# Projections of the first cross-attention in half chunks, one to a tile, and ten tiles of its softmax sums on POOL

## The reference

```python
cq = heads(ci @ cq_w, NH, CHD)            # 16 heads of 8
ckv = encoder_outputs @ ckv_w
ck, cv = jnp.split(ckv, 2, axis=-1)
ck, cv = (heads(ck, NH, CHD), heads(cv, NH, CHD))
cctx = sdpa(cq, ck, cv, causal=False)     # softmax(cq ck / sqrt(8)) cv
```

## Time and profile before

| | us |
|---|---|
| median of 3 runs (lowest, highest) | 1729.5 (1728.61, 1733.84) |
| the profiled execution | 1730.58 |
| its span | 1728.8 |
| PE busy | 1527.6 (88%) |
| DVE busy | 976.1 (56%) |
| ACT busy | 621.7 (36%) |
| POOL busy | 473.5 (27%) |
| loop of the first cross-attention, in the span | 242.8 to about 658 |

### The profile page before, as it was taken

How to read it: one execution, slowest core, us unless ns; L and a number is a source line. 1 busy time by engine, 2 the same in 40 slices (tenths; PEclk the granted TensorE clock), 3 DMA queues, 4 the chain that set the end, 5 groups by cost and what they waited for, 6 DMA issues and landing times.

```text
span 1728.8 us, 22247 instructions
## 1 busy us (share of the span) xinstructions
PE 1527.6 (88%) x8274; PEld 795.9 (46%) x8275; DVE 976.1 (56%) x1410; ACT 621.7 (36%) x997; POOL 473.5 (27%) x377
## 2 busy tenths in 40 slices
PE   7667569999999988998996789999899989999998
PEld 3234225455454444445663335555434345555344
DVE  6775456666666735412334657677542667777541
ACT  1132226655656652003553223333313233333221
POOL 1540025665665761000000104333000123343000
PEclk9877569999999998998998889999999999999999
DMA  6000512232232214002311000110012100000000
GB/s 234 0 1 3 117 36 66 70 90 65 70 90 57 62 28 127 0 0 72 108 71 53 32 0 27 31 33 19 2 33 68 58 9 28 27 28 19 3 0 22
DMA packets 37829, 80.42 MB, mean 47 GB/s; under 512 B 5564, under 2 KB 23756, under 8 KB 37708
## 3 DMA queue, kind: packets, MB, share of 16 engines
q1 hardware_dynamic: 37712, 78.91, 15.7%
HBM read 56.79 MB, written 0.92 MB: 33 GB/s over the span
## 4 chain that ended last, share of the span: by engine, by line
PE 73%; DVE 17%; ACT 4%; issue 3%; POOL 1%; DMA 0%; SPq 0%; DVEq 0%; POOLq 0%; ACTq 0%
PE psum L1722 20%; PE psum L2242 7%; DVE WA L1386 5%; PE psum L1888 4%; PE psum L1914 3%; PE psum L1939 3%; PE psum L2189 3%; PE psum L1861 3%; DVE WBZ L1625 3%; PE psum L2057 3%; PE psum L1874 3%; PE psum L2217 2%; PE psum L2219 2%; PE psum L2250 2%; PE psum L2234 2%
## 5 line engine op out<-in xcount | busy, mean ns | idle before, releaser
L1386 DVE TENSOR_REDUCE WA<-psum 112x2 f32<-112x1000 f32 x192 | 230.5, 1200 | 141.3 <-PE psum L1888 141.1
L953 ACT ACTIVATE WBZ<-psum 125x896 f32<-125x896 f32 x192 | 176.0, 917 | 158.0 <-PE psum L1914 122.2
L1116 ACT ACTIVATE WA<-psum,y_bias 125x448 f32<-125x448 f32 x192 | 121.4, 634 | 253.5 <-PE psum L2237 253.5
L740 POOL TENSOR_TENSOR XN<-XN,WBZ 125x896 f32<-125x896 f32 x96 | 199.9, 2082 | 15.3 <-ACT WBZ L953 1.8
L2242 PE MATMUL psum<-WA,ctxN 125*128 125x448 f32 x384 | 179.1, 550 | 0.4 <-ACT WA L1116 0.4
L1613 DVE TENSOR_REDUCE y_max<-psum 112x1 bf16<-112x375 f32 x256 | 129.8, 538 | 65.3 <-PE psum L2219 65.0
L769 POOL TENSOR_TENSOR XN<-const,y_max 112x896 bf16<-112x896 f32 x32 | 53.7, 1679 | 335.2 <-DVE y_max L1613 326.5
L1888 PE MATMUL psum<-WA,XB 32*112 32x500 f16 x384 | 84.6, 435 | 39.8 <-DVE WA L1386 39.8
L1914 PE MATMUL psum<-R 100*125 100x224 f16 x768 | 116.3, 274 | 0.0
L760 POOL TENSOR_SCALAR ctxT<-ctxT 128x375 f32<-128x375 f32 x32 | 56.1, 1754 | 199.1 <-ACT std L839 196.5
L1625 DVE RECIPROCAL WBZ<-WBZ 128x224 f32<-128x224 f32 x68 | 105.1, 1547 | 1.2
(11 more groups left out here) (257 smaller groups left out, 2630.1 us busy)
## 6 DMA issues: line engine op xcount, KB each, us to landing
R<-WA SPq DMA_DIRECT2D x192, 93.8 KB, 2.2
ctxT<-in_ctxT SPq DMA_DIRECT2D x12, 750.0 KB, 4.3
R<-in_ctxT SPq DMA_DIRECT2D x12, 750.0 KB, 5.5
WA<-in_ctxT SPq DMA_DIRECT2D x8, 750.0 KB, 4.1
ctxT<-in_ctxT SPq DMA_DIRECT2D x32, 187.5 KB
ctxN<-in_ctx SPq DMA_DIRECT2D x32, 187.5 KB
WBZ<-in_x_w SPq DMA_DIRECT2D x4, 1024.0 KB, 6.4
WA<-in_x_wq SPq DMA_DIRECT2D x2, 1024.0 KB, 6.7
```

Of the source, the lines that this page charges most:

```text
L740: nc.gpsimd.tensor_tensor(z_sum[b % 2][0:TK, :], first[0:TK, :], z_p[t % 4][0:TK, :], ALU.add)\
L953: nc.scalar.activation(z_p[t % 4][0:TK, :].rearrange("p (k n) -> p k n", k=2), psum[0:TK, s:s + 2, 0:2 * GC], ACT.Exp, scale=float(CHD0) * ...
L1116: nc.scalar.activation(y_pT[t][0:TK, g * HALF:(g + 1) * HALF], bank[2 + u % 3][0:TK, 0:HALF], ACT.Exp, bias=y_bias[0:TK, bass.ds(b * NT + ...
L1386: V.tensor_reduce(z_mx[0:PR, r:r + 3:2, c], psum[0:PR, 4:6, 0:PC], AX_X, ALU.max)\
```

## The change

Each projection is cut into two halves, side 0 and side 1, one to a tile: the values in tiles 0 to 5, the keys in tiles 6, 7, 9, 10 and 11 and, for the last half, between the first and the second group of `sums`. Side 0 stands behind the tile's `scores`, side 1 ahead of them, and only side 1 signals ACT. ACT empties the bank ahead of the exponent of the next tile. `turn_maxima` keeps tile 8 for itself. `UNITS_AT` goes from 5 to 4, so each unit comes one tile later. `SUMS` goes from 7 to 9: POOL adds tiles 0 to 9 with nine adds, PE has three groups of sums, and the waits of `exps` for a free buffer change with it. The diff, cut to its core:

```diff
-        UNITS_AT = 5
-        VALUES_AT = {0: 0, 1: 1, 3: 2}
-        KEYS_AT = {4: 0, 6: 1, 9: 2}
-        LOW_AT = {5: 0, 7: 1, 10: 2}
+        UNITS_AT = 4
+        VALUES_AT = {0: (0, 0), 1: (0, 1), 2: (1, 0), 3: (1, 1), 4: (2, 0), 5: (2, 1)}
+        KEYS_AT = {6: (0, 0), 7: (0, 1), 9: (1, 0), 10: (1, 1), 11: (2, 0), 12: (2, 1)}
         TURN_AT = 8
-        SUMS = NT - 5
+        SUMS = NT - 3
...
+                elif b > 0 and t < SUMS - 7:
+                    act.wait_ge(sem("z_pv"), g - 3)
+                    act.wait_ge(sem("z_sums"), SUMS * (b - 1) + 8 + t)
                 elif b > 0:
-                    act.wait_ge(sem("z_added"), ADDED * (b - 1) + t + 1)
+                    act.wait_ge(sem("z_added"), ADDED * (b - 1) + t - (SUMS - 7) + 1)
...
+                    if b + 1 < B and t in VALUES_AT and VALUES_AT[t][1] == 1:
+                        values(b + 1, VALUES_AT[t][0])
+                    if b + 2 < B and t in KEYS_AT and KEYS_AT[t][1] == 1:
+                        high_keys(b + 2, KEYS_AT[t][0])
                     if t + 1 < NT:
                         exps(b, t + 1)
...
-                    if b + 1 < B and t in VALUES_AT:
-                        values(b + 1, VALUES_AT[t])
-                    if b + 2 < B and t in KEYS_AT:
-                        high_keys(b + 2, KEYS_AT[t])
+                if b + 2 < B:
+                    high_keys(b + 2, PIECES - 1)
...
-                    if b + 2 < B and t in LOW_AT:
-                        low_keys(b + 2, LOW_AT[t])
+                    if b + 2 < B and t in KEYS_AT and KEYS_AT[t][1] == 1:
+                        low_keys(b + 2, KEYS_AT[t][0])
                     if b > 0 and t == 3:
                         divide(b - 1)
+                if b + 2 < B:
+                    low_keys(b + 2, PIECES - 1)
...
+                at = slice(side * (PC // 2), (side + 1) * (PC // 2))
+                mm = pe.matmul(bank[7][:, at], w_ck, z_ctx[b % 2][:, c * PC:(c + 1) * PC][:, at], start=True, stop=True)
+                if side == 1:
+                    mm.then_inc(sem("z_k"), 1)
...
-                for j in range(4):
+                for j in range(2 * side, 2 * side + 2):
...
-                    pe.wait_ge(sem("z_kl"), PIECES * (b + 1) + (2 if b > 0 else 3))
+                    pe.wait_ge(sem("z_kl"), PIECES * (b + 1) + (1 if b > 0 else PIECES))
...
+                    for turn in range(2):
+                        if b + 1 < B and t in VALUES_AT and VALUES_AT[t][1] != turn:
+                            values(b + 1, *VALUES_AT[t])
+                        if b + 2 < B and t in KEYS_AT and KEYS_AT[t][1] != turn:
+                            keys(b + 2, *KEYS_AT[t])
+                        if turn == 0 and t + 1 < NT:
+                            scores(b, t + 1)
+                        elif turn == 0 and b + 1 < B:
+                            scores(b + 1, 0)
                     if b + 1 < B and t == TURN_AT:
                         turn_maxima(b + 1)
...
-                sums(b)
+                sums(b, 0)
+                if b + 2 < B:
+                    keys(b + 2, *KEYS_AT[NT])
+                for i in range(1, ADDED):
+                    sums(b, i)
```

More of the change, by code:

```diff
@@ L1848, in _, with keys @@
                 product(("cq", h), [(w_cq[:, k], XN[:, k, half(h)]) for k in range(KD)])
-            def keys(b, c):
-                if c == 0:
+            def keys(b, c, side):
+                if side == 0 and c == 0:
                     pe.wait_ge(sem(f"z_ctx{b % 2}"), 16 * (b // 2 + 1))
@@ L1856, in keys, with values @@
                         pe.wait_ge(sem("z_values"), PIECES * b)
-                else:
+                elif side == 0:
                     pe.wait_ge(sem("z_kl"), PIECES * b + c)
[L1859 to L1866, removed]
+                    if c == 1 and b > 1:
+                        pe.wait_ge(sem("z_shifts"), b)
+                at = slice(side * (PC // 2), (side + 1) * (PC // 2))
+                mm = pe.matmul(bank[7][:, at], w_ck, z_ctx[b % 2][:, c * PC:(c + 1) * PC][:, at], start=True, stop=True)
+                if side == 1:
+                    mm.then_inc(sem("z_k"), 1)
+            def values(b, c, side):
+                if side == 0 and c == 0:
                     pe.wait_ge(sem("z_kl"), PIECES * (b + 1))
@@ L1875, in values @@
                                    start=True, stop=True)
-                mm.then_inc(sem("z_v"), 1)
+                if side == 1:
+                    mm.then_inc(sem("z_v"), 1)
             def unit(b, k):
@@ L1916, in scores, with sums @@
                 mm.then_inc(sem("z_scores"), 1)
[L1918 to L1927, removed]
+            def sums(b, i):
+                if i == ADDED - 1:
+                    pe.wait_ge(sem("z_sums"), SUMS * (b + 1))
+                part = z_p[(SUMS + 1 + i) % 4] if i < ADDED - 1 else z_sum[b % 2]
+                for g in range(QG):
+                    mm = pe.matmul(bank[6][g * GR:(g + 1) * GR, GC:2 * GC], z_ones[0:TK, :],
+                                   part[0:TK, g * GC:(g + 1) * GC], start=(i == 0), stop=(i == ADDED - 1))
+                mm.then_inc(sem("z_added"), 1)
             def attended(b, t):
@@ L1946, in _ @@
             for c in range(PIECES):
-                keys(0, c)
+                for side in range(2):
+                    keys(0, c, side)
             for c in range(PIECES):
-                values(0, c)
+                for side in range(2):
+                    values(0, c, side)
             for c in range(PIECES):
-                keys(1, c)
+                for side in range(2):
+                    keys(1, c, side)
             pe.wait_ge(sem("z_split"), 2)
```

## The result

The changed kernel takes 1758.83 us (1757.85 to 1765.82, 4 runs) against 1729.05 before (4 runs): ratio 1.0178, 95% interval 1.0143 to 1.0212. It is 30 us slower; 10 faster was forecast, with a range up to 1731. The profiled execution is the longest of the four (1765.82, span 1764.0), 35.2 us above the span before; the other three are 7 to 8 us shorter, and have no trace.

The account below looks back on a forecast made before the run. PE was taken as the bound, with holes. Thirteen batches -8.4 us, one unit less ahead of the loop -2.0, batch 0 -1.4 and batch 14 +1.4 gave -10.4: 1719.1 us against 1729.5, range 1707 to 1731.

Parts of the forecast that it names:

- Rival A: Tile 5's floor gives way: product costs 1.04 us wherever it starts, T5 at 9.9, 1708 us in all; chance 0.1.
- the tile of the turn: Tile 8, where `turn_maxima` stands: DVE's `combine` and `low_keys` set the start of its maximum; 1.98 us to T9.
- The two groups of sums: End of each batch on PE: two of the groups of sums go, 0.38 us each, -0.76 a batch.
- the nine adds hide in full batches: POOL's nine adds are done at 22.6 us and needed at T0 + 25.1, so the two more are covered.
- Batch 14: Little work for PE, so POOL's nine adds bound it: 23.2 us instead of 21.80, +1.4 us.
- the one of tiles 0 to 5: Evened tiles of 1.84 us; product still ends at 9.50, T5 stays at 10.7, gain 0.2 us, PE stands about 1.5.
- the edges: Outside the full batches: one unit less ahead of the loop -2.0 us, batch 0 -1.4, batch 14 +1.4, batch 15 0.
- the sums with the half of keys: End of a batch: 2.0 us now, less 0.76 for two groups, plus 0.43 for the half and 0.10: 1.78 us.
- The changes of kind: Two switches between kinds of matmul, around the half of keys among the sums: 0.10 us together.
- Rival B: Small new waits eat the evened tiles, 0.1 us to spare at `turn_maxima` and tile 11: 1724 us; chance 0.17.
- rival C: Slower: a split projection exposes a weight load on seven halves behind T5, +0.7 us a batch: 1738 us; chance 0.11.

Follow-up runs that it names:

- the first experiment: The changed kernel with DVE's division (reciprocal and product) behind the maximum of tile 5 instead of tile 3: 1720.86 us, ratio 0.9956 against the kernel before.
- the sixth run: The changed kernel with the division at tile 5, and the last half of keys moved from among the sums into tile 11: 1715.62 us, ratio 0.9929.

## Why the prediction was wrong

*What held.* The product of the division meets the same add, grows to 1.84 (1.9 forecast), T5 stays at T0 + 10.66 (10.7), PE stands still for 1.31 (about 1.5). Rival A is refuted, and with it pricing the product by its mean. From T5 to T10: 437.76 - 428.10 = 9.66, against 1.84 + 2 x 1.82 + 1.98 + 2.10 = 9.56 by the steps; of these the tile of the turn came 0.20 shorter (433.68 to 435.46) and the tile behind it 0.20 longer. The two groups of sums are worth 0.76, and the nine adds hide in full batches.

*What came near for another reason.* Batch 14 takes 24.02 (23.2 forecast), but POOL doesn't end it here: with the clock at 0.50 from 657.7 to 664.6 PE comes late itself and nowhere waits for POOL. Where the clock stays up, PE does wait for it as forecast, 2.06 us in the first experiment and 2.07 with the nine adds alone. And the prediction named three of PE's waits for DVE in a batch before; a fourth, of 0.25 us, stands ahead of tile 6. Its sum doesn't use it.

*The step that failed* is the one of tiles 0 to 5: "PE stands still for about 1.5 us ahead of T5", priced as a gain that doesn't come, at nothing more. It was taken for certain that batches 1 to 13 would run at the 1.00 that the earlier trace rows show for them. But those rows are of a PE whose longest wait was 0.35. The clock answers to the standing still of 1.3 us: up to 2 us behind it, in three batches of thirteen, it halves and stays so for 20 to 24 us, +29.1 us in the profiled execution (106.82 for the three, against 77.73). In the runs without the hole (division two tiles later, product on POOL, hole filled) it stays at 1.00 in all thirteen. Why three batches and not thirteen is open.

The same fault is in the edges: "it starts in the slow clock: 28.31 now, about 26.9" took the moment at which the clock rises as given. It rises at 278.9 instead of 247.4. In the kernel before it rose behind the first whole chunk of values (eight records, 244.20 to 246.14); with the nine adds alone, which keep that tile, it rose at 247.1. The half that stands there now doesn't raise it. That is +16 us against the forecast of batch 0.

*A term of the wrong size*: the sums with the half of keys, 1.78 forecast, 2.00 measured. The changes of kind were put at 0.10 together and cost 0.33, shown by the sixth run. The tiles with a half ahead of `scores` take 1.86 to 1.88 instead of 1.82 to 1.84. Together they make 25.91 out of the forecast 25.56, 4.5 us in 13 batches. At a full clock that would still have been 0.30 a batch faster than before, 4 us.

The whole distance from the forecast of -10.4 to the +35.2 of the profiled execution is 45.6 us, made up, to the rounding, of 29.1 from the falls, 16.3 from batch 0, 4.5 from the longer batches, 0.8 from batch 14, less 4.7 upstream and 0.3 behind the stage.

Rival B's small waits and rival C's weight loads did not decide: the only waits from tile 5 to the end of a batch are those priced, and in the tiles a half costs 0.01 to 0.05 more than its share. Whether weight loads are part of the 0.33 among the sums is open. None of the rivals had the mechanism that decided. Two rows ahead of the prediction pointed at it: in the earlier trace rows a PE with a wait of 1.30 us runs at the slow clock (0.66 us for a unit that takes 0.42 otherwise), and batch 0 at 0.92 in the earlier trace rows began in it. The range of any step that leaves PE standing should have included the other clock for the stretch behind it.

TensorE: Matmul & The Clock Gate of the Trainium skill, in its section on psum-queue cycling, tells of something near: frequent short idle times between groups of matmuls make the clock swing, and throughput is lost to that. The trace agrees, with one idle time of 1.31 us to a batch and 20 to 24 us at 0.50 behind three of them.

## What to carry to other kernels

A wait on PE has two prices: its own length and, once it is long enough, the granted clock of the stretch behind it (here 1.3 us cost 8.7 to 10.2 us in each of the three batches that it hit, while 1.0 us cost only itself). So evening out work on PE in front of a fixed release gathers several small waits into one large one of the same sum (1.58 us a batch here), and that can be worse than the uneven list. Move the release away (1720.9 us); filling the hole gave less (1739.6). Look in the trace for short two-input instructions of DVE whose length varies: if they end with an instruction of POOL, move them to where an add ends, or give them to POOL.

## What the runs showed of the hardware that was not expected

- PE at 1.2 GHz and busy without a gap does not soon get its clock back: it was busy 43.16 of 43.17 us in batch 0 of the changed kernel, and the clock stood at 0.50 until 278.9, 0.4 us before the end. With eight records of 128x125 float32 products more, in one tile, it rose 3 us behind the first of them. What in the work counts for it was not taken apart.
- Batches with the same wait fare differently within one execution: of thirteen the clock fell in 3, 8 and 13 in the changed kernel (343.7, 480.3 and 620.2 us), and in 2 to 13 with the halves alone, every 30.7 us. What picks them was not found.
- A DVE product of 128x56 from two tiles of on-chip memory took 0.22 us with POOL idle and 0.33 to 1.84 us by when it was issued within an add of POOL. It didn't delay the adds: with the product among them eight take 17.65 us, 2.21 each, as the 13.21 for six before.
